# LayerNorm ahead of an attention block: the normalising instruction moved from VectorE to GpSimd

## The reference

```python
def _layernorm(x, axis=-1, eps=1e-5):
    m = jnp.mean(x, axis=axis, keepdims=True)
    v = jnp.var(x, axis=axis, keepdims=True)
    return (x - m) / jnp.sqrt(v + eps)

xn = _layernorm(x, axis=-1)
s = _L0_attn_ref(xn, ...)          # 16 heads, 4 k/v heads, rms norm, rope, low-rank bias
g = _silu(_L0_ffn_ref(xn, ...))    # 2048 -> 5632 (gate, up) -> 2048
x = x + s * g
```

## Time and profile before

| | us |
|---|---|
| median of 2 runs (4542.52 to 4544.97) | 4543.74 |
| the profiled execution | 4549.63 |
| its span on the slowest core, core 5 | 4548.1 |
| spans of the eight cores | 4520.8 to 4548.1 |
| busy on core 5: PE | 3606.0 (79%) |
| VectorE | 1121.6 (25%) |
| ScalarE | 908.4 (20%) |
| GpSimd | 391.0 (9%) |

### The profile page before, as it was taken

How to read it: one execution, slowest core, us unless ns; L and a number is a source line. 1 busy time by engine, 2 the same in 40 slices (tenths; PEclk the granted TensorE clock), 3 DMA queues, 4 the chain that set the end, 5 groups by cost and what they waited for, 6 DMA issues and landing times. The chain is left out here.

```text
span 4548.1 us, 38839 instructions; the slowest of 8 cores (4520.8 to 4548.1 us)
## 1 busy us (share of the span) xinstructions
PE 3606.0 (79%) x15274; PEld 1491.5 (33%) x15274; DVE 1121.6 (25%) x1179; ACT 908.4 (20%) x895; POOL 391.0 (9%) x343
## 2 busy tenths in 40 slices
PE   1576577786999998888999999873677887886973
PEld 1222222222444443333444444331122222322433
DVE  7122124342000000000100000004444455552006
ACT  2121023331000000000000000001344444542112
POOL 0000012111111110001111110000000000000000
PEclk9976888887999999999999999996788888987986
DMA  3211232123877774556788755542000000003348
GB/s 131 57 18 19 83 54 37 31 35 42 80 76 74 75 74 70 75 77 76 75 78 79 75 63 77 74 81 90 21 19 20 17 17 17 6 17 93 37 113 280
DMA packets 547235, 287.85 MB, mean 63 GB/s; under 512 B 457075, under 2 KB 528756, under 8 KB 540020
## 3 DMA queue, kind: packets, MB, share of 16 engines
q0 software_dynamic: 498480, 162.55, 34.1%
q1 hardware_dynamic: 48580, 122.82, 7.9%
HBM read 397.53 MB, written 50.33 MB: 98 GB/s over the span
## 5 line engine op out<-in xcount | busy, mean ns | idle before, releaser
L900 PE MATMUL p_dps<-p_hfm,p_dwb 128*128 128x512 bf16 x2816 | 628.1, 386 | 89.0 <-ACT p_gout L918 58.8
L828 PE MATMUL p_gps<-xn_fm,p_gwb 128*128 128x512 bf16 x2816 | 625.5, 380 | 37.1 <-DMA p_uwb<-wu 37.1
L835 PE MATMUL p_ups<-xn_fm,p_uwb 128*128 128x512 bf16 x2816 | 622.1, 379 | 0.0
L861 DVE SCALAR_TENSOR_TENSOR p_hfm<-p_ups,c_ups,p_sg 128x1024 bf16<-128x1024 f32 x88 | 113.0, 1284 | 1499.4 <-ACT p_sg L850 1499.4
L1299 ACT ACTIVATE p_ptb<-p_scr,st_bnegb 128x1024 bf16<-128x1024 f32 x320 | 367.6, 1151 | 497.2 <-DVE p_scr L1250 351.8
L1155 PE MATMUL p_sc<-p_qg,p_kfm 128*128 128x512 bf16 x640 | 285.9, 464 | 188.8 <-DVE p_ogs L1231 97.3
L900 PEld LDWEIGHTS p_dps<-p_hfm,p_dwb 128*128 128x128 bf16 x2816 | 277.5, 99 | 439.5 <-issue 122.8
L828 PEld LDWEIGHTS p_gps<-xn_fm,p_gwb 128*128 128x128 bf16 x2816 | 276.0, 98 | 373.3 <-issue 44.4
L835 PEld LDWEIGHTS p_ups<-xn_fm,p_uwb 128*128 128x128 bf16 x2816 | 275.6, 98 | 332.2
L697 PE MATMUL p_qps<-xn_fm,p_wbuf 128*128 128x512 bf16 x1024 | 290.1, 441 | 37.0 <-DMA p_wbuf<-wq 37.0
L850 ACT ACTIVATE p_sg<-p_gps,c_gates 128x1024 f32<-128x1024 f32 x88 | 98.2, 1116 | 1090.7 <-PE p_ups L835 1090.7
(11 more groups left out here) (140 smaller groups left out, 2651.2 us busy)
## 6 DMA issues: line engine op xcount, KB each, us to landing
p_gwb<-wg POOLq DMA_DIRECT2D x88, 512.0 KB, 8.4
p_uwb<-wu POOLq DMA_DIRECT2D x88, 512.0 KB, 10.3
p_dwb<-wd POOLq DMA_DIRECT2D x88, 512.0 KB, 5.7
p_xt<-x SPq DMA_DIRECT2D x32, 1024.0 KB, 7.1
y<-p_outb SPq DMA_DIRECT2D x16, 1024.0 KB, 10.4
p_wbuf<-wq POOLq DMA_DIRECT2D x16, 512.0 KB, 6.4
sp_q<-p_qout SPq DMA_DIRECT2D x64, 128.0 KB, 1.8
sp_g<-p_gout SPq DMA_DIRECT2D x32, 256.0 KB, 3.0
```

The source lines that it names most:

```text
L828: tensor.matmul(gps[:, po + q4 * 512:po + (q4 + 1) * 512], gw_[:, ec * 128:(ec + 1) * 128], xn_cols(ec, hh * 1024 + q4 * 512, 512), start= ...
L835: mm = tensor.matmul(ups[:, po + q4 * 512:po + (q4 + 1) * 512], uw_[:, ec * 128:(ec + 1) * 128], xn_cols(ec, hh * 1024 + q4 * 512, 512), s ...
L861: vector.scalar_tensor_tensor(hfm[:, ic * 1024:(ic + 1) * 1024], ups[:, po:po + 1024], ups_c[:, ic:ic + 1], sg[:, po:po + 1024], ALU.mult, ...
L900: mm = tensor.matmul(dps[:, oc4 * 1024 + q4 * 512: oc4 * 1024 + (q4 + 1) * 512], wv_[:, oc4 * 128:(oc4 + 1) * 128], hfm[:, ic * 1024 + q4 ...
```

## The change

The normalising instruction of p0 goes from VectorE's program to a new program for GpSimd, with the waits that it had (aR, aT) and the same operands. VectorE goes on to the next tile's statistics as soon as those of this one are done; from the third tile on it waits for aX of the tile two back. `st0` gets 16 columns, and even and odd tiles use eight each, on all three engines that touch it. SyncE's and PE's programs stay as they are.

```diff
-                st0 = sb("p0_st", [128, 8], F32)
+                st0 = sb("p0_st", [128, 16], F32)
...
                     def _(vector):
                         for tt in range(NTT):
+                            b = (tt % 2) * 8
                             xv = xt[:, (tt % 2) * E:(tt % 2) * E + E]
                             vector.wait_ge(aLp[tt % 2].h, 16 * (tt // 2 + 1))
-                            vector.reduce_sum(st0[:, 0:1], xv, AX.X)
+                            if tt >= 2:
+                                vector.wait_ge(aX.h, tt - 1)
+                            vector.reduce_sum(st0[:, b + 0:b + 1], xv, AX.X)
                             vector.scalar_tensor_tensor(
                                 xsq[:, :], xv, 1.0, xv, ALU.bypass, ALU.mult,
-                                accum_out=st0[:, 1:2])
+                                accum_out=st0[:, b + 1:b + 2])
...
-                            vector.tensor_tensor(st0[:, 5:6], st0[:, 4:5], st0[:, 3:4], ALU.subtract).then_inc(aS.h, 1)
+                            vector.tensor_tensor(st0[:, b + 5:b + 6], st0[:, b + 4:b + 5], st0[:, b + 3:b + 4], ALU.subtract).then_inc(aS.h, 1)
                             aS.inc()
-                            vector.wait_ge(aR.h, tt + 1)
+
+                    @block.gpsimd
+                    def _(gpsimd):
+                        for tt in range(NTT):
+                            b = (tt % 2) * 8
+                            xv = xt[:, (tt % 2) * E:(tt % 2) * E + E]
+                            gpsimd.wait_ge(aR.h, tt + 1)
                             if tt >= 1:
-                                vector.wait_ge(aT.h, tt)
-                            vector.tensor_scalar(
-                                xnt[:, :], xv, st0[:, 2:3], st0[:, 6:7],
+                                gpsimd.wait_ge(aT.h, tt)
+                            gpsimd.tensor_scalar(
+                                xnt[:, :], xv, st0[:, b + 2:b + 3], st0[:, b + 6:b + 7],
                                 ALU.subtract, ALU.mult).then_inc(aX.h, 1)
                             aX.inc()
...
-                            scalar.activation(st0[:, 7:8], st0[:, 5:6], AF.Ln, bias=EPS_LN)
+                            scalar.activation(st0[:, b + 7:b + 8], st0[:, b + 5:b + 6], AF.Ln, bias=EPS_LN)
                             scalar.drain()
-                            scalar.activation(st0[:, 6:7], st0[:, 7:8], AF.Exp, scale=-0.5).then_inc(aR.h, 1)
+                            scalar.activation(st0[:, b + 6:b + 7], st0[:, b + 7:b + 8], AF.Exp, scale=-0.5).then_inc(aR.h, 1)
```

More of the change, by code:

```diff
@@ L190, in _ @@
                                 xsq[:, :], xv, 1.0, xv, ALU.bypass, ALU.mult,
-                                accum_out=st0[:, 1:2])
+                                accum_out=st0[:, b + 1:b + 2])
                             vector.drain()
-                            vector.tensor_scalar(st0[:, 2:3], st0[:, 0:1], 1.0 / E, None, ALU.mult)
-                            vector.tensor_scalar(st0[:, 4:5], st0[:, 1:2], 1.0 / E, None, ALU.mult)
+                            vector.tensor_scalar(st0[:, b + 2:b + 3], st0[:, b + 0:b + 1], 1.0 / E, None, ALU.mult)
@@ L195, in _ @@
+                            vector.tensor_scalar(st0[:, b + 4:b + 5], st0[:, b + 1:b + 2], 1.0 / E, None, ALU.mult)
                             vector.drain()
-                            vector.tensor_tensor(st0[:, 3:4], st0[:, 2:3], st0[:, 2:3], ALU.mult)
+                            vector.tensor_tensor(st0[:, b + 3:b + 4], st0[:, b + 2:b + 3], st0[:, b + 2:b + 3], ALU.mult)
                             vector.drain()
-                            vector.tensor_tensor(st0[:, 5:6], st0[:, 4:5], st0[:, 3:4], ALU.subtract).then_inc(aS.h, 1)
+                            vector.tensor_tensor(st0[:, b + 5:b + 6], st0[:, b + 4:b + 5], st0[:, b + 3:b + 4], ALU.subtract).then_inc(aS.h, 1)
```

## The result

The change makes the kernel slower by 0.9%: the ratio of the changed kernel's time to that of the kernel before is 1.0087 (95% interval 1.0061 to 1.0113), so 28 to 51 us, 40 at the middle. The forecast was +17 us, 4561, with a range to 4605; the median over all runs of the changed kernel is 4607.6. That median, and the 4593.3 of the runs of the kernel before made beside it, hold executions in which one die ran at a lower clock; the ratio leaves them out, and what follows goes by it. The direction was right and the change stays within 2%, but the size was out by more than a factor of two.

The account below looks back on a forecast made before the run. VectorE's chain was taken to bound p0 at 7.31 us a tile; with X at 4.68 us on GpSimd the xt buffer loop gives 8.35, ending p0 17 us later: 4543.7 becomes 4561 us, range 4538 to 4605.

Parts of the forecast that it names:

- steps 1 and 5: p0: VectorE's chain falls from 7.31 to 5.25 us a tile, gain at most 33 us; added wait and banks cost nothing.
- step 2: X on GpSimd in p0: duration T taken as 4.68 us from a tensor_tensor row, range 1.35 to 9.36.
- step 3: p0's two xt buffers: next load waits for X, so a tile costs 6.01 + T/2, 8.35 us; this loop decides.
- 9T - 25.1: Change in p0's end in us, with T the time of X on GpSimd, for T up to 7.4; forecast 17 later.
- gaps all equal to T + 2.3: Sign of being wrong: tile gaps in p0 set by GpSimd's own loop, T being X's time there.
- step 4: p0's single xnt: next X waits for the transposes, T + 2.3 a tile, 7.0 us; takes over from T = 7.4.
- the cost beside it: p0: X and VectorE's two-input sum of squares may exclude one another; p0 then ends 21 us later rather than 17.
- T + 3.85: Least time of a p0 tile if the sum of squares waits for X's end; 8.53 us at T = 4.68.
- A quick GpSimd: Rival: X takes 1.35 to 3.5 us on GpSimd, change of -13 to +6 us, time 4531 to 4550; chance 0.25.
- GpSimd as the bound: Rival: X, transposes, X on single xnt bounds p0, kernel over 2% slower, from T = 10.5 without exclusion; chance 0.06.
- exclusion or slow GpSimd, +30 to +91: Rival: GpSimd and VectorE exclude one another in p0, or X is slow, costing +30 to +91 us; chance 0.18.
- The most likely case: X takes 3.5 to 6 us, xt's buffer loop sets p0, little or no exclusion; 4550 to 4573 us; chance 0.5.

Follow-up runs that it names:

- e1: Changed kernel with X (the normalising instruction) back on VectorE, st0 banks and aX wait kept; ratio to the kernel before 1.0001.
- e5: Changed kernel with GpSimd running eight instruction forms in turn in place of X; tensor_scalar 7.09 us with two steps, 5.38 with one, tensor_tensor 3.60, copy 1.89.
- e6: Changed kernel with X on 1024 of 2048 columns, the rest zeroed once; X 3.78 us, barrier behind p0 at 148.3 and 148.9 us, no ratio.
- e3: Changed kernel with two xnt buffers and Ln waiting for the X two tiles back; barrier behind p0 at 177.5 us on the mean, against 181.7; no ratio.
- e2: Changed kernel with four xt buffers in place of two; ratio to the kernel before 1.0159, barrier behind p0 at 208.5 and 209.3 us.
- e9: Changed kernel with four xt, two xnt, Ln waiting for X two tiles back, and one-pass bn_stats/bn_aggr statistics on VectorE; ratio to the kernel before 0.9999.
- e10: Changed kernel with four xt buffers and one-pass bn_stats/bn_aggr statistics on VectorE; ratio to the kernel before 1.0075.
- e7: Kernel before plus two tiny GpSimd tensor_scalars in p0, the second behind tile 14; both took 1.43 us.
- e11: Kernel before plus two tiny GpSimd tensor_scalars in p0, the second behind the last X; that second one took 0.37 us.

## Why the prediction was right or wrong

*What bounds the kernel, the stage, the other edits (steps 1 and 5).* Right. e1 shows the other edits at nothing, p0 is longer by 42.8 us on the mean of the cores where the ratio gives 40 (28 to 51), and PE's wait behind it is no longer than before. The prediction takes 2% for what a measurement of this kernel can tell; the interval here is half a percent wide.

*The price of X (step 2).* This is the step that failed: 4.68 taken, 7.24 measured. The mistake was in what I took as nearest. I chose tensor_tensor's rate for each element, and argued about the number of inputs. e5 shows that the kind of instruction decides (with one step 5.38 for tensor_scalar, 3.60 for tensor_tensor) and that a second step adds 1.7. The doubling for the second step, my own upper end 9.36, was the nearer of the two corrections, though the step didn't double the time. The Trainium skill's "GPSIMD Engine Reference", Engine selection, that one-input work is roughly line-rate, holds here for the copy, 1.89 us, and is far off for tensor_scalar, 5.4 and 7.2. The estimate of 1.7 us for X that I drew from it was 4 times too low.

*The buffer's loop (step 3) and the formula.* The loop is real, e6 and e3 show its pairs, but it isn't the one that decided. With T mis-sized the path came out wrong too: at 7.24 and loads of 4.9 us the buffer's loop asks for 9.1 a tile, and GpSimd's own for 9.54. The prediction named this as a sign of being wrong (gaps all equal to T + 2.3), and it is what most gaps show; the forecast pairs of 7.0 and 9.7 didn't come. That 9T - 25.1 still gives +40.0 at 7.24 is because the two loops cross at 7.4, and the +8.9 at 3.78 is in part luck, as said under e6. A core with quicker loads was to lose 8 us less; at the barrier the cores stand at 180.3 to 183.6, 3 us apart. With the two loops so close, undoing one could gain little: e3 gained 4 us, and e2 was even worse.

*GpSimd's own loop (step 4).* Its price was right, T + 2.3: X waits 2.30 us for the transposes in 10 of 16 tiles on core 1, and on core 3, with loads of 4.9 us, all but 2 of the gaps behind the first are 9.53. The step had it take over only from T = 7.4, with loads of 5.9.

*Exclusion (the cost beside it).* It exists, and I had its price for the change nearly right (2.1 us, in the first tile, where I had put 4) and its rule wrong. The form T + 3.85 a tile would have given 11.1 us at T = 7.24; L192 and X hardly meet in the changed kernel, and if they do, VectorE is held for X's first 4.50 us only. One such meeting in the changed kernel, on core 3:

```profile
110.64 7.24 POOL L212 TENSOR_SCALAR p_xnt<-p_xt,p_st 128x2048 bf16<-128x2048 f32 x1 [3.25 <-ACT p_st L226]
...
114.57 2.85 DVE L192 SCALAR_TENSOR_TENSOR p_xsq<-p_xt 128x2048 f32<-128x2048 f32 x1
```

L192 took 2.85 in place of 2.28, released at 117.42 - 2.28 = 115.14, again 4.50 us behind X. The other way about, a VectorE instruction that is first keeps GpSimd waiting to its end: 2.1 us in the first tile and in each of e2. The Trainium skill's "SBUF — State Buffer", Who interferes with whom, is borne out in that the two exclude one another with two SBUF inputs on VectorE, by who comes first, and that the reduce, bn_stats and L196, with one, go through (e2, e9, e10). Its "for the whole instruction", which it says of VectorE's 2-port modes and which I took for two inputs as well, is not borne out where X comes first: 4.5 of its 7.24.

*The rivals.* A quick GpSimd is refuted by e5. GpSimd as the bound, the chain X, transposes, X, is the mechanism that came, at +39 by its own form; over 2% needed T = 10.5. The case "exclusion or slow GpSimd, +30 to +91" held 0.18 of my chance, and that is where it fell. The most likely case should have been wider, since its T came from a row of another instruction.

*What I had not foreseen.* That more buffers could cost time (e2): they move VectorE's instruction onto the start of X.

## What to carry to other kernels

A duration on GpSimd must come from a row of the same instruction with the same number of arithmetic steps; a row of another instruction, even with more inputs, is no bound from above. An instruction that leaves an engine keeps its place in every loop of buffers: write each loop as a sum (issue, landing, the readers, X) before looking at which engine is relieved. And before moving work off a busy engine, ask whether the work can be halved there: one pass over the data instead of two gained 36 us in p0, where the move lost 40.

## What the runs showed of the hardware

- tensor_scalar on GpSimd, 128x2048, f32 to bf16: 7.24 us with two steps, 5.4 with one, 3.79 for 1024 columns with two; a copy 1.89. VectorE takes 1.35 for the two steps.
- Such an instruction holds off VectorE's instructions with two SBUF inputs for its first 4.5 us, even one of a single column (L199, 4.00 us instead of 0.16). tensor_tensor on GpSimd (3.60 us) held off L192 of e5 until 3.46 us behind its start. VectorE's reduce (2.29 us), its bn_stats (a median 676 ns) and its one-column instructions with one input (0.15) ran beside X unhindered.
- Where VectorE's two-input instruction started 0.01 or 0.10 us behind X's recorded start, VectorE went first and X was 2.1 us longer. At 1.36 us and more behind, X went first.
- A tensor_scalar of 128x2 on GpSimd took 1.43 us where VectorE's tensor_scalar of 128x2048 (1.35 us) started beside it, and 0.37 where that had ended (e7, e11).
- The V matmuls ran at 437 ns on two cores and at 379 on six in one execution of the changed kernel, at granted clocks of 0.82 and 1.00. What brings it stays open.
